# Attention scores made a second time with keys on the partitions, their row maxima subtracted in PSUM by matmuls

## The reference, cut to what matters

```
q = _qdq(layernorm(x)) @ _qdq(wq).T + bq          # _qdq: int8 fake quantization along the last axis
kv = cond @ wkv.T + bkv ;  k, v = split(kv)
attn = softmax(einsum('bnhd,bmhd->bhnm', q, k) * scale, axis=-1)
o = einsum('bhnm,bmhd->bnhd', attn, v)
x = x + tanh(g_xattn[1]) * (_qdq(o) @ _qdq(wp).T + bp)
```

## Time and profile before

| | us |
|---|---|
| median of 3 runs (lowest, highest) | 222.12 (220.98, 223.53) |
| the profiled execution | 223.4 |
| its span | 221.0 |
| busy: TensorE, VectorE | 182.7, 173.1 |
| busy: ScalarE, POOL | 101.7, 87.7 |
| mean granted TensorE clock | 0.965 of 2.4 GHz |

### The profile page before, as it was taken

How to read it: one execution, slowest core, us unless ns; L and a number is a source line. 1 busy time by engine, 2 the same in 40 slices (tenths; PEclk the granted TensorE clock), 3 DMA queues, 4 the chain that set the end, 5 groups by cost and what they waited for, 6 DMA issues and landing times.

```text
span 221.0 us, 3793 instructions
## 1 busy us (share of the span) xinstructions
PE 182.7 (83%) x1284; PEld 118.8 (54%) x1284; DVE 173.1 (78%) x465; ACT 101.7 (46%) x256; POOL 87.7 (40%) x130
## 2 busy tenths in 40 slices
PE   0369999989989989785877778797687789999992
PEld 0236555567655556441555546574566357756761
DVE  0798999984178999979789999999956853775674
ACT  2440352212332335721467758775686562633531
POOL 1485657043855521663320204420120453663720
PEclk9999999999999999995599999999999969999998
DMA  6979870000000000000000000000000000002002
GB/s 184 395 220 374 323 263 0 3 0 0 0 0 1 3 1 0 0 0 1 3 0 3 1 3 0 3 0 4 0 0 3 1 0 3 0 0 69 29 0 95
DMA packets 5729, 10.98 MB, mean 50 GB/s; under 512 B 752, under 2 KB 4432, under 8 KB 5200
## 3 DMA queue, kind: packets, MB, share of 16 engines
q1 hardware_dynamic: 5072, 9.74, 12.8%
q10 hardware_dynamic: 640, 1.02, 1.2%
HBM read 9.68 MB, written 1.07 MB: 49 GB/s over the span
## 4 chain that ended last, share of the span: by engine, by line
PE 54%; DVE 26%; issue 9%; ACT 5%; DMA 4%; SPq 0%; DVEq 0%
PE PS L1606 9%; PE PS L1266 5%; PE PS L1268 5%; PE PS L1267 5%; PE PS L1624 5%; DVE R L992 5%; DMA X<-x 4%; DVE SM L983 4%; PE PS L1354 4%; PE PS L1588 3%; PE PS L1330 3%; PE PS L1288 3%; PE PS L1297 2%; DVE T_R L921 2%; PE PS L1542 2%
## 5 line engine op out<-in xcount | busy, mean ns | idle before, releaser
L472 POOL TENSOR_SCALAR T_R<-QT,SM 128x256 bf16<-128x256 f32 x48 | 22.4, 484 | 27.3 <-DVE SM L1060 15.0
L983 DVE TENSOR_REDUCE SM<-PS 128x8 f32<-128x1024 f32 x16 | 18.8, 1214 | 2.6 <-PE PS L1429 1.5
L1440 PE MATMUL PS<-CON,R 128*128 128x128 f32 x128 | 18.9, 281 | 1.2 <-ACT R L617 1.2
L450 POOL TENSOR_TENSOR R<-R,CON 128x256 f32<-128x256 f32 x16 | 9.6, 621 | 25.7 <-PE PS L1429 16.5
L736 ACT ACTIVATE R<-PS 128x512 f32<-128x512 f32 x17 | 10.1, 596 | 19.5 <-PE PS L1606 19.4
L617 ACT ACTIVATE R<-PS 128x512 f32<-128x512 f32 x32 | 18.2, 593 | 1.5 <-PE PS L1440 1.4
L992 DVE TENSOR_TENSOR R<-PS,SM 128x1024 f32<-128x1024 f32 x16 | 18.8, 1214 | 0.0
L334 POOL TENSOR_TENSOR R<-CT 128x512 f32<-128x512 f32 x12 | 13.5, 1126 | 12.9 <-PE PS L1268 7.6
L1221 DVE TENSOR_TENSOR R<-R,PS 128x512 bf16<-128x512 f32 (+1 forms) x17 | 11.7, 686 | 8.2 <-ACT R L736 5.4
L525 ACT ACTIVATE LNV<-MV,EPSC 128x1 f32<-128x1 f32 (+1 forms) x26 | 7.5, 290 | 22.4 <-DVE MV L906 11.1
L1606 PE MATMUL PS<-T_R,R 128*128 128x512 bf16 x64 | 17.1, 388 | 0.4 <-DVE T_R L1159 0.4
(11 more groups left out here) (153 smaller groups left out, 433.7 us busy)
## 6 DMA issues: line engine op xcount, KB each, us to landing
WST<-w SPq DMA_DIRECT2D x3, 1024.0 KB, 11.4
T_R<-lagged SPq DMA_DIRECT2D x2, 768.0 KB, 7.9
X<-x SPq DMA_DIRECT2D x2, 512.0 KB, 6.7
CT<-ctxr SPq DMA_DIRECT2D x1, 1024.0 KB, 7.4
y<-X SPq DMA_DIRECT2D x8, 128.0 KB, 1.8
WKV<-wkv SPq DMA_DIRECT2D x1, 512.0 KB, 9.9
WQP<-wqp ACTq DMA_DIRECT2D x1, 512.0 KB, 6.3
R<-sw SPq DMA_DIRECT2D x3, 128.0 KB, 4.5
```

What stands on the lines that cost most here:

```text
L472: nc.gpsimd.tensor_scalar(XB[:, u % 2, j, :], MX[:, b, :], GG[:, b, e:e + 1], 1.0, ALU.mult, ALU.mult).then_inc(e_xb, 1)
L983: V_.tensor_reduce(MX1[:, b % 2, 8 * c:8 * c + 8], S4[:, 8 * c:8 * c + 8, :], AX.X, ALU.max).then_inc(a_mx, 1)
L1440: ins = TR(PS[:, 4 + k % 2, P * h:P * h + P], SS[:, b % 2, 4 * k + h, :], I)
```

## The change

- a_subtract and the buffer SS go, and with them a_turn.
- The scores are made twice. a_scores(b, half) makes each block's scores with queries on the partitions in two halves of two row groups, for the maxima alone. a_turned(b, i) makes the same scores with keys on the partitions, straight into bank 2 + i, for row group TURN[i]: two float32 matmuls of 32 rows against 256 columns a call, four calls a block. Its moving operand QBD is the masked double of the queries, made by block_queries on POOL.
- a_parts (VectorE) writes the 16 maxima of each query to MXP as two bfloat16 parts; a_top turns MXP (TensorE), a_maxima copies it out as MXT (ScalarE), and a_shift(b, i) adds minus the maximum to the open accumulation: four bfloat16 matmuls a call, with SEL (ones times minus one in the two rows of the wanted head) as weights and MXT as moving operand. SEL is made once by four operations on POOL from four more columns of the constants.
- The exponentials read banks 2 to 5. Banks 2 and 3 are used by both: the second score half of block s+1 waits for the first two exponentials of block s.
- The loops hold one block less between scores and end: o_norm(s-1), o_rows(s-1), o_transpose(s-2), m_transpose(s-4), a_exp(s). LATE goes from 3 to 2. In the tail turned(0) stands before finish(NB - 1), and the gates of the first group before the last o_norm.

```diff
@@ POOL
+            def block_queries(b):
+                pool.wait_ge(a_q, 2 * (b + 1))
+                if b >= 2:
+                    pool.wait_ge(a_et, 4 * (b - 1))
+                for c in range(2):
+                    nc.gpsimd.tensor_tensor(QBD[:, b % 2, c], AQH[:, b % 2, c, :].unsqueeze(1).to_broadcast([P, 2, P]),
+                                            MASK.unsqueeze(2).to_broadcast([P, 2, P]), ALU.mult).then_inc(qbd, 1)
...
             for b in range(2, NB):
                 block_keys(b)
                 if b < 4:
                     bias_rows(b + NB - 4)
-                if b >= 5:
-                    finish(b - 5)
+                block_queries(b)
+                if b >= 4:
+                    finish(b - 4)
@@ ScalarE
-            def a_exp(b, k):
-                act.wait_ge(a_et, 4 * b + k + 1)
-                nc.scalar.activation(ET[:, b % 2, 4 * k:4 * k + 4, :],
-                                     PS[:, 4 + k % 2, :].rearrange("p (h n) -> p h n", h=4), ACT.Exp
+            def a_maxima(b):
+                act.wait_ge(a_tx, b + 1)
+                nc.scalar.copy(MXT, PS[:, 3, 0:P // 2].bitcast(BF16)).then_inc(a_xt, 1)
+
+            def a_exp(b, i):
+                r = TURN[i]
+                act.wait_ge(a_et, 4 * b + i + 1)
+                nc.scalar.activation(ET[:, b % 2, 4 * r:4 * r + 4, :],
+                                     PS[:, 2 + i, :].rearrange("p (h n) -> p h n", h=4), ACT.Exp
                                      ).then_inc(a_ex, 1)
...
                 if s + 2 < NB:
                     a_zt_(s + 2)
                 if s >= 1:
-                    a_exp(s - 1, 0)
-                if s >= 5:
-                    m_rstd(s - 5)
-                if s >= 3:
-                    o_q_(s - 3)
+                    o_pe_(s - 1)
+                if s >= 4:
+                    m_rstd(s - 4)
                 if s + 2 < NB:
                     a_q0_(s + 2)
-                if s >= 1:
-                    a_exp(s - 1, 1)
+                a_maxima(s)
                 if s + 2 < NB:
                     a_q_(s + 2)
...
+                a_exp(s, 0)
+                a_exp(s, 1)
+                if s >= 2:
+                    o_ev_(s - 2)
+                a_exp(s, 2)
+                if s + 4 < NB:
+                    a_rstd(s + 4)
+                a_exp(s, 3)
+                if s >= 2:
+                    o_y_(s - 2)
                 if s >= 1:
...
+                    o_q_(s - 1)
                 if s + 3 < NB:
                     a_zq_(s + 3)
...
+                if s >= 4:
+                    m_zt_(s - 4)
@@ VectorE
-            def a_subtract(b, c):
...
-                V_.tensor_tensor(SS[:, a, ks, :], S4[:, ks, :], MX1[:, a, ks].unsqueeze(2).to_broadcast([P, 8, P]),
-                                 ALU.subtract).then_inc(a_sub, 1)
+            def a_parts(b):
+                m = MX1[:, b % 2, :].rearrange("p (r j) -> p r j", r=4)
+                hi, mid = (MXS[:, :, 0:4, n:n + 1].rearrange("p r i t -> p r (i t)") for n in range(2))
...
+                dve.wait_ge(a_mx, 2 * b + 2)
+                s_mp.mark(V_.tensor_copy(hi, m))
+                s_mp.wait()
+                s_mp.mark(V_.tensor_tensor(mid, m, hi, ALU.subtract))
@@ TensorE
+            def a_scores(b, half):
+                pe.wait_ge(a_q, 2 * (b + 1))
+                pe.wait_ge(kbd, 2 * (b + 1))
+                if b == 0:
+                    pe.wait_ge((x1, f_me)[half], (NB, NB - 1)[half])
+                else:
+                    pe.wait_ge((a_mx, a_ex)[half], (2 * b - 1, 4 * b - 2)[half])
                 for c in range(2):
                     for r in (2 * half, 2 * half + 1):
...
+            def a_turned(b, i):
+                r = TURN[i]
+                rows = slice(VW * r, VW * r + VW)
+                if i < 2:
+                    pe.wait_ge(a_mx, 2 * b + 2)
+                elif b >= 1:
+                    pe.wait_ge(a_ex, 4 * (b - 1) + i + 1)
...
+                if i == 1:
+                    pe.wait_ge(a_xt, b + 1)
+                pe.wait_ge(qbd, 2 * (b + 1))
+                for c in range(2):
+                    M(PS[:, 2 + i, 2 * P * c:2 * P * c + 2 * P], KT[rows, c, b, :],
+                      QBD[rows, b % 2, c].rearrange("p s n -> p (s n)"), start=(c == 0), stop=False,
+                      skip_group_check=True)
+
+            def a_top(b):
+                pe.wait_ge(a_mp, 2 * (b + 1))
+                TR(PS[:, 3, 0:P // 2].bitcast(BF16), MXP, IDB[:, :]).then_inc(a_tx, 1)
+
+            def a_shift(b, i):
+                r = TURN[i]
+                rows = slice(VW * r, VW * r + VW)
...
+                pe.wait_ge(a_xt, b + 1)
+                for j in range(4):
+                    ins = M(PS[:, 2 + i, P * j:P * j + P], SEL[rows, j, :], MXT[rows, :], start=False, stop=True,
+                            skip_group_check=True)
                 ins.then_inc(a_et, 1)
...
             for s in range(NB):
-                if s >= 1:
-                    a_turn(s - 1, 0)
                 if s + 2 < NB:
                     a_transpose(s + 2)
...
                 if s >= 1:
                     a_values(s - 1, 0)
                     a_values(s - 1, 2)
+                a_turned(s, 2)
+                a_turned(s, 3)
+                if s + 2 < NB:
+                    a_project(s + 2)
+                if s + 1 < NB:
+                    a_scores(s + 1, 0)
                 if s >= 1:
+                    o_rows(s - 1)
+                a_turned(s, 0)
+                a_top(s)
+                if s + 2 < NB:
+                    a_q_transpose(s + 2)
+                a_turned(s, 1)
+                for i in range(4):
+                    a_shift(s, i)
+                if s >= 2:
+                    o_transpose(s - 2)
+                if s + 1 < NB:
+                    a_scores(s + 1, 1)
+                a_values(s, 1)
+                a_values(s, 3)
+                if s >= 2:
+                    o_project(s - 2)
+                if s >= 4:
+                    m_transpose(s - 4)
```

More of the change, by code:

```diff
@@ L268, in build @@
             "a_q"))
-        a_s0 = sem("a_s0")
-        a_s, a_mx, a_sub, a_et, a_ex, a_pv = (sem(n) for n in (
+        a_s, a_mx, a_mp, a_tx, a_xt, a_et, a_ex, a_pv = (sem(n) for n in (
             "a_s",
             "a_mx",
-            "a_sub",
+            "a_mp",
+            "a_tx",
+            "a_xt",
             "a_et",
@@ L495, in _ @@
             block_keys(1)
-            for b in range(NB - 2):
+            for j in range(4):
+                nc.gpsimd.tensor_scalar(SEL[:, j, :], ONES[:, :], SELC[:, j:j + 1], 1.0, ALU.mult, ALU.mult
+                                        ).then_inc(sel, 1)
+            for b in range(NB - 3):
                 bias_rows(b)
+            block_queries(0)
+            bias_rows(NB - 3)
+            block_queries(1)
             pool.wait_ge(v_dg, 3)
@@ L1066, in _ @@
                     a_max(0, 1)
-                    a_subtract(0, 0)
+                    a_parts(0)
                 if route:
@@ L1109, in _ @@
             for s in range(NB):
-                norm, new, moe = s >= 2, s + 3 < NB, s >= 4
+                norm, new, moe = s >= 1, s + 3 < NB, s >= 3
                 if s >= 1:
@@ L1113, in _ @@
                     a_max(s, 1)
-                    a_subtract(s, 0)
-                a_subtract(s, 1)
-                if new and s >= 1:
-                    a_stats(s + 3, 0)
-                if norm:
-                    o_norm(s - 2, 0)
-                if new and s >= 1:
-                    a_stats(s + 3, 1)
-                if norm:
-                    o_norm(s - 2, 1)
-                if norm:
-                    o_norm(s - 2, 2)
-                if s >= 5:
-                    m_rows(s - 5)
-                if norm:
-                    o_norm(s - 2, 3)
+                    a_parts(s)
                 if new:
@@ L1162, in _ @@
             dve.wait_ge(ones_s, 3)
-            o_norm(NB - 2, 0)
-            m_rows(NB - 5)
-            o_norm(NB - 2, 1)
-            m_stats(NB - 4, 0)
-            o_norm(NB - 2, 2)
-            m_stats(NB - 4, 1)
-            for k in range(3, 6):
-                o_norm(NB - 2, k)
-            finish(NB - 3)
-            o_norm(NB - 1, 0)
+            m_gates(0, 0)
+            m_gates(0, 1)
+            o_norm(NB - 1, 0)
+            m_gates(0, 2)
+            o_norm(NB - 1, 1)
+            m_gates(0, 3)
+            o_norm(NB - 1, 2)
+            m_gates(0, 4)
+            o_norm(NB - 1, 3)
+            m_gates(0, 5)
+            o_norm(NB - 1, 4)
             m_rows(NB - 4)
-            o_norm(NB - 1, 1)
+            o_norm(NB - 1, 5)
             m_stats(NB - 3, 0)
-            o_norm(NB - 1, 2)
             m_stats(NB - 3, 1)
-            for k in range(3, 6):
-                o_norm(NB - 1, k)
             finish(NB - 2)
             m_stats(NB - 2, 0)
-            m_gates(0, 0)
-            m_gates(0, 1)
             m_stats(NB - 2, 1)
-            m_gates(0, 2)
```

(25 more changed lines are left out.)

169 lines of the change are left out of this document (62 added, 107 removed).

## The result

The changed kernel takes 299.94 us (median of 4 runs, 298.31 to 300.06), beside 222.39 for the kernel before (4 runs, 220.98 to 223.53): a ratio of 1.346, 95% interval 1.339 to 1.353. The forecast was 245.0 with a range of 233 to 256. The sign was right, the size was not: the change costs 77.5 us where I had 23.

The account below looks back on a forecast made before the run. VectorE set the stage before; TensorE was to become the bound, gaining net 2.9 us a block against 1.4 of air. Iterations and tail summed to +23, span 221.0 to 244, median 245, range 233 to 256.

Parts of the forecast that it names:

- the clock: In iteration 0 of the attention loop, TensorE's clock returns to full at about 107 us, bounds 105 and 110.
- rival C: Whole kernel slower by more, 253 us: pair 1.5, shifts 0.9, half clock until 110 and again in the tail; 17%.
- score half, start to next start: On TensorE, each of a block's two score halves takes 1.08 us, together 1.08 more than before.
- lone a_turned: On TensorE, a_turned calls 0 and 1, with other tilings between them, cost 1.06 us each.
- pair of a_turned: On TensorE, a_turned calls 2 and 3 in succession cost 1.3 us, between 1.1 side by side and 1.5.
- a_top to a_turned 1: On TensorE, a_turned 1 waits for ScalarE's copy of a_top: 0.55 us with a_q_transpose inside.
- a_turned 1 and the shifts: On TensorE, a_turned 1 at 1.06 us plus a block's sixteen bfloat16 shift matmuls at 0.5 (0.35 to 0.9).
- wait before the second half: On TensorE, the second score half waits for the block before's exponentials 0 and 1: 0.7 us stays uncovered.
- TensorE ready until a_zq is done: At the next iteration's start, a_transpose waits for a_zq while TensorE is ready: 1.3 us in iterations 2 to 4.
- the stage: One full stage of the attention loop at full clock, 9.7 + 1.3 = 11.0 us.
- A: Whole kernel faster: TensorE hides the added work between its waits, VectorE's 15.8 us come out, 206 us; 4%.
- B: Whole kernel slower by less, 235 us: same bound, stalls vanish, pair and shifts at lower bounds, turned(0) free; 25%.

Follow-up runs that it names:

- experiment 1: The changed kernel plus 24 whole-array float32 matmuls once, ahead of the loop: 301.81 us.
- experiment 2: The changed kernel plus 8 and 4 extra float32 matmuls of 128 rows in each iteration from the second, where TensorE waits: 273.41 us.
- experiment 3: The changed kernel plus 8 and 4 extra float32 matmuls of 32 rows in each iteration from the second, where TensorE waits: 325.28 us.
- experiment 10: The kernel before plus 16 extra float32 matmuls of 32 rows in each of seven iterations: 249.99 us.
- experiment 11: The kernel before plus 16 extra float32 matmuls of 128 rows in each of seven iterations: 236.88 us.
- experiment 9: The changed kernel plus extra whole-array float32 matmuls at 100 us, in the waits of the iterations from the second and in the tail: 273.75 us.
- experiment 5: The kernel before with only each block's scores split into two halves of two row groups: 224.48 us, ratio 1.012.

## Why the prediction was right in its sign and wrong in its size

The step that failed is the clock. "TensorE being busier, I let the clock return at about 107; bounds 105 and 110", and in rival C "a stage with TensorE busy 6.6 of 8 us kept the full clock, and the new ones are denser". It returned at about 246, in the tail, behind 3.6 us of the experts' whole-array float32 matmuls (L1631), and was lost once more from about 254 to 261 (0.55). I had read the clock off the busy share and did not ask what the busy time was made of. Before, 32-row matmuls in float32 were one burst a block with all four row groups at work, 1.15 us of 8; the change made them five bursts of one or two groups a stage (the pair is two calls side by side), mostly with nothing beside them, and took the whole-array turns away. Each of these calls is fully busy in the records and leaves half or three quarters of the rows without work. Experiments 1 to 3 show that this mix, and neither the late start nor the stalls, holds the clock at 1.2 GHz; 10 and 11 show the same of extra matmuls in the kernel before, and that no stall is needed for the fall. Whether stalls hasten the fall in the changed kernel is open: in experiments 1 and 9 it came within 2 us after the first one.

That this is all of the excess in the loop's middle is borne out by the stage of experiment 2, and so is the rest of the working, term by term (us, at full clock, from its timeline):

| term | forecast | measured |
|---|---|---|
| score half, start to next start | 1.08 | 1.07 |
| lone a_turned | 1.06 | 1.06 |
| pair of a_turned | 1.3 (1.1 to 1.5) | 1.07 |
| a_top to a_turned 1 | 0.55 | 0.63 |
| a_turned 1 and the shifts | 1.06 + 0.5 | 1.29 |
| wait before the second half | 0.7 | 0.9 |
| TensorE ready until a_zq is done | 1.3 | 1.3 |
| the stage | 11.0 | 11.05, fillers taken off |

Pair and shifts came out 0.2 to 0.3 us lower each, the way to a_turned 1 and the wait for the exponential 0.1 and 0.2 higher. That the total is met within 0.1 is partly luck.

- VectorE: 7.97 - 5.93 = 2.04 us a block saved, forecast 2.0. Right, and worth nothing, as said: TensorE sets the stage. VectorE's largest waits are for L1430 and L1491.
- The ordering inside the stage, the new wait for the exponential and the chain o_project, o_y, o_q, a_zq, a_transpose stand in the trace as forecast, at 0.55 and 1.18 us since ScalarE's durations do not double with TensorE's.
- POOL's added work cost nothing: none of TensorE's waits in the changed kernel is put down to POOL.
- Of the rivals, A was refuted by the stage of 11 us at full clock, and B and C were both variants of a kernel at full clock. C named the right quantity and gave it 2.5 us at the loop's start and 1 us in the tail (where the second loss did come); it needed a case in which the clock does not return at all. That costs 6.7 us a stage (17.77 against 11.05) and 40 over the six; I could have priced it from the earlier trace rows, where TensorE's work at half clock stood before me, and did not, because I took the return of the clock in the kernel before for a property of any busy loop.
- The Trainium skill, "TensorE: Matmul & The Clock Gate", Part 2 (step 1), keeps matmuls in program order, and I set 1.5 for the pair, 0.9 for the shifts and 250 us against my own number by it. The trace disagrees: the pair takes 1.07 as one call does, and a_turned 1 with the shifts behind it 1.29.

Open: the changed kernel was never seen at full clock throughout. A stage of 11.05 where 11.0 was forecast supports a total near 245 for that case, but iteration 7 and the tail were not tested in the same way. How much of the array's rows the work has to fill was not settled either: 64 rows in the fillers did not do and 128 did, in these places. The change also took the turns away, and that was not tested apart from the calls that it added; experiment 10 shows only that such calls bring the clock down with the turns in place. And all the 32-row calls that were added or packed were float32; nothing was tried with bfloat16 ones.

## What to carry to other kernels

Before moving work onto TensorE, read the shapes of the matmuls as well as the busy share: calls that fill one or two of four row groups look as busy as any and can cost the whole loop half its clock, which nearly doubles every other matmul too. Forecast such a change twice, once at each of the two clock levels, and let the range hold both. Adding whole-array work bought part of it back (from 300 us to 273 with twelve calls a stage, and no lower with up to nineteen), and never enough to make the change pay.

## What the runs showed of the hardware that was not expected

- TensorE stayed at 1.2 GHz for 140 us while it was busy 90% (the changed kernel) and 98% (experiment 3), and kept 2.4 GHz over 57 us at 90% (experiment 5). The Trainium skill, "TensorE: Matmul & The Clock Gate", Part 1, describes the gate by how busy the array has recently been; if that is read as the busy share of a profile, these windows disagree with it.
- Row groups overlap across calls, not only within a block that was written for it. In the changed kernel a score half (two groups) and the a_turned that follows it (a third group, other PSUM bank) run in the same four waves, here the first:

```profile
106.46 0.80 PE L1430 MATMUL PS<-R 32*128 32x256 f32 x2
106.48 0.79 PE L1448 MATMUL PS<-R 32*128 32x256 f32 x1
```

  Both together took 2.03 us at half clock, to the a_top at 108.49, where either alone takes 2.0 to the next start.
- A float32 matmul against 128 columns costs the same with 32 rows as with 128 at a given clock (3.83 and 3.79 us for sixteen, experiments 10 and 11). Rows left empty saved nothing.
